# The sums of a wide step: copied by ScalarE and added by GpSimd instead of added by VectorE

## The reference

```python
# layers 0, 2 (wide)
q, k, v = hidden @ Wq, ctx @ Wk, ctx @ Wv            # 16 heads of 64
logits = einsum('bhqd,bhkd->bhqk', q, k) * 64 ** -0.5 + col_bias
probs = softmax(logits, axis=-1)
out = einsum('bhqk,bhkd->bhqd', probs, v)
x = out.reshape(B, HW, 1024) @ Wo + bo + x
# layers 1, 3 (narrow)
xn = rmsnorm(x, norm_w)                              # 16 heads of 16, 4 key/value heads
attn = softmax(einsum('btgrd,bsgd->bgrts', q, k) * 16 ** -0.5, axis=-1)
x = x + einsum('bgrts,bsgd->btgrd', attn, v) @ wo
```

## Time and profile before

| | |
|---|---|
| median of 3 runs | 1727.05 us (1723.91 to 1731.9) |
| profiled execution | 1724.81 us, span 1722.6 us |
| mean granted TensorE clock | 0.967 |
| TensorE (PE) busy | 1599.6 us, 93% |
| VectorE (DVE) busy | 1250.8 us, 73% |
| ScalarE (ACT) busy | 1015.1 us, 59% |
| GpSimd (POOL) busy | 476.2 us, 28% |

### The profile page before, as it was taken

How to read it: one execution, slowest core, us unless ns; L and a number is a source line. 1 busy time by engine, 2 the same in 40 slices (tenths; PEclk the granted TensorE clock), 3 DMA queues, 4 the chain that set the end, 5 groups by cost and what they waited for, 6 DMA issues and landing times.

```text
span 1722.6 us, 29786 instructions
## 1 busy us (share of the span) xinstructions
PE 1599.6 (93%) x10732; PEld 889.0 (52%) x10732; DVE 1250.8 (73%) x2376; ACT 1015.1 (59%) x1721; POOL 476.2 (28%) x354
## 2 busy tenths in 40 slices
PE   7998798999999999999999999999999999999884
PEld 6886444454545454545454454545464545454443
DVE  5474467687878787878777877778787878786551
ACT  2111176667666676667666765676667666666452
POOL 5342402122232322323213222221323132322221
PEclk9898799999999999999999999999999999999886
DMA  7988412241225131513262224322341224030332
GB/s 259 329 298 264 142 33 62 53 83 46 62 49 117 28 85 36 130 26 96 71 135 77 66 60 93 67 56 59 77 87 34 77 57 106 28 88 18 99 112 64
DMA packets 176738, 160.57 MB, mean 93 GB/s; under 512 B 91722, under 2 KB 133066, under 8 KB 175570
## 3 DMA queue, kind: packets, MB, share of 16 engines
q1 hardware_dynamic: 174410, 150.21, 33.3%
q10 hardware_dynamic: 2184, 8.47, 1.2%
HBM read 115.11 MB, written 43.48 MB: 92 GB/s over the span
## 4 chain that ended last, share of the span: by engine, by line
PE 57%; DVE 11%; issue 11%; POOL 4%; ACT 4%; DMA 1%; SPq 1%; ACTq 0%; POOLq 0%; DVEq 0%
PE general L1534 10%; PE general L1653 10%; PE score_ps L1593 5%; PE score_ps L1594 5%; PE out_ps L1608 5%; PE general L1551 3%; PE general L1555 3%; PE general L1613 3%; PE out_ps L1619 3%; PE out_ps L1629 3%; POOL kept L1394 2%; PE score_ps L1582 2%; DVE q_aux L1436 2%; DVE q_aux L1435 2%; DVE a_lo L1470 2%
## 5 line engine op out<-in xcount | busy, mean ns | idle before, releaser
L1445 DVE TENSOR_REDUCE tops<-general 128x2 bf16<-128x308 f32 x1024 | 427.3, 469 | 55.9 <-PE general L1551 33.5
L1289 ACT ACTIVATE probs<-score_ps 128x512 f32<-128x512 f32 x512 | 297.8, 598 | 112.0 <-PE score_ps L1594 100.7
L1394 POOL TENSOR_TENSOR kept<-kept,inv_b 128x512 f32<-128x512 f32 x128 | 171.1, 1358 | 463.0 <-DMA inv_b<-scratch_inverses 463.0
L1432 DVE TENSOR_TENSOR q_pair<-general,q_pair 64x512 fp32r<-64x512 f32 x160 | 109.5, 684 | 168.0 <-ACT q_pair L1277 164.2
L1301 ACT ACTIVATE q_aux<-general 4x512 bf16<-4x512 bf16 x320 | 187.6, 586 | 20.0 <-PE general L1564 15.0
L1276 ACT ACTIVATE q_pair<-general 64x512 fp32r<-64x512 f32 x160 | 94.6, 591 | 154.3 <-PE general L1534 123.7
L1313 ACT ACTIVATE kept<-out_ps 128x512 f32<-128x512 f32 x192 | 104.3, 595 | 85.4 <-PE general L1623 67.0
L1384 POOL TENSOR_TENSOR x_lo<-xn,x_hi 128x1024 fp32r<-128x1024 f32 x31 | 74.0, 2388 | 282.2 <-ACT x_hi L1257 217.7
L1332 ACT ACTIVATE a_hi<-kept 128x512 fp32r<-128x512 f32 x160 | 93.6, 625 | 97.5 <-PE general L1653 49.5
L1594 PE MATMUL score_ps<-q_pair,w_pair 128*128 128x512 f32 x256 | 149.5, 592 | 0.0
L1470 DVE TENSOR_TENSOR a_lo<-kept,a_hi 128x512 fp32r<-128x512 f32 x160 | 125.0, 813 | 32.7 <-ACT a_hi L1332 31.7
(11 more groups left out here) (158 smaller groups left out, 3295.8 us busy)
## 6 DMA issues: line engine op xcount, KB each, us to landing
inv_b<-scratch_inverses SPq DMA_DIRECT2D x128, 256.0 KB, 4.7
w_pair<-scratch_wk_hi SPq DMA_DIRECT2D x32, 256.0 KB, 6.8
x<-scratch_stream SPq DMA_DIRECT2D x16, 512.0 KB, 3.3
inv_n<-scratch_inverses SPq DMA_DIRECT2D x256, 32.0 KB, 1.8
xn<-scratch_stream SPq DMA_DIRECT2D x15, 512.0 KB, 3.3
scratch_stream<-x SPq DMA_DIRECT2D x14, 512.0 KB, 4.6
scratch_wk_hi<-p_kout_hi SPq DMA_DIRECT2D x16, 308.0 KB
p_raw<-in_L_xattn_Wk_dram SPq DMA_DIRECT2D x4, 1024.0 KB, 7.9
```

What stands on the lines that cost most here:

```text
L1289: nc.scalar.activation(dst, score_ps[:, number % 2, :], ACT.Exp, scale=scale).then_inc(act_exp.sem, 1)
L1394: last = nc.gpsimd.tensor_tensor(tiles[i], tiles[i], (inv_b, inv_n)[n % 2][:, i, :], ALU.mult)
L1445: last = nc.vector.tensor_reduce(tops[:, n % 2, sub, 2 * pair:2 * pair + 2], src, AX_X, ALU.max)
```

## The change

For every wide step, ScalarE copies the bank of sums to one of two tiles, `step_sums`, right after its two copies to `kept`. For the second to the fourth step of a chunk GpSimd adds: at the second the two tiles into `wide_sums`, then each next tile to `wide_sums`. VectorE does nothing in `value`. TensorE waits for ScalarE's copy before it uses the bank again, SyncE waits for GpSimd's third addition before it stores the sums, and ScalarE waits, before it fills a tile, for the addition that read the tile last. PLAN is the same.

```diff
-        wide_sums = sb("wide_sums", [P, TOK])
+        wide_sums, step_sums = sb("wide_sums", [P, TOK]), sb("step_sums", [P, 2, TOK])
...
-        dve_sums = Signal(sem("dve_sums"), ("value",), only=WIDE_STEPS, parts=(1,))
+        act_sums = Signal(sem("act_sums"), ("value",), only=WIDE_STEPS, parts=(1,))
+        pool_sums = Signal(sem("pool_sums"), ("value",), only=[n for n in WIDE_STEPS if n % 4], parts=(1,))
...
-        reader = {"value": dve_sums, "query": dve_query, "max": dve_max, "turn": act_turn, "output": dve_output,
+        reader = {"value": act_sums, "query": dve_query, "max": dve_max, "turn": act_turn, "output": dve_output,
...
-                            wait(sp, dve_sums.sem, dve_sums.after(w, "value", 4 * c + 3, 1))
+                            wait(sp, pool_sums.sem, pool_sums.after(w, "value", 4 * c + 3, 1))
...
                         nc.scalar.activation(kept[:, place(tile), :], out_ps[:, tile % 2, :], ACT.Copy).then_inc(act_keep.sem, 1)
+                    if wide(n):
+                        if n % 4 > 1:
+                            before_w, before = it, n - n % 4 + 1
+                        else:
+                            before_w, before = (it, n - 8 + 2) if n >= 8 else (it - 1, n + 8 + 2)
+                        wait(act, pool_sums.sem, pool_sums.after(before_w, what, before, 1))
+                        ps = bank_of((it, what, n, k, 0))
+                        nc.scalar.activation(step_sums[:, n % 2, :], ps, ACT.Copy).then_inc(act_sums.sem, 1)
...
+                elif what == "value":
+
+                    if not wide(n) or k == 0 or n % 4 == 0:
+                        return
+                    wait(pool, act_sums.sem, act_sums.after(it, what, n, k))
+                    if n % 4 == 1:
+                        wait(pool, sums_stored.sem, sums_stored.after(it - (n == 1), "sums", 2 - n // 4, 0))
+                        first = step_sums[:, 0, :]
+                    else:
+                        wait(pool, pool_sums.sem, pool_sums.after(it, what, n - 1, k))
+                        first = wide_sums[:]
+                    nc.gpsimd.tensor_tensor(wide_sums[:], first, step_sums[:, n % 2, :], ALU.add).then_inc(pool_sums.sem, 1)
...
-                elif what == "value":
-
-                    if not wide(n) or k == 0:
-                        return
-                    wait(dve, pe_value.sem, pe_value.after(it, what, n, k))
-                    ps = bank_of((it, what, n, k, 0))
-                    if n % 4 == 0:
-                        wait(dve, sums_stored.sem, sums_stored.after(it - (n == 0), "sums", 2 - n // 4, 0))
-                        nc.vector.tensor_copy(wide_sums[:], ps).then_inc(dve_sums.sem, 1)
-                    else:
-                        wait(dve, dve_sums.sem, dve_sums.after(it, what, n - 1, 1))
-                        nc.vector.tensor_tensor(wide_sums[:], ps, wide_sums[:], ALU.add).then_inc(dve_sums.sem, 1)
```

## The result

The changed kernel took 1761.14 us (median of 4 runs, 1755.24 to 1764.65), the kernel before 1726.33 us in 4 runs beside it. The ratio is 1.0189 with an interval of 1.0164 to 1.0214: about 33 us slower, where 28 were forecast (the two medians are 35 us apart).

The account below looks back on a forecast made before the run. The prediction took TensorE, busy 192.24 of 200 us in a middle stretch, as the bound. It summed 27.5 + 2 + 4 + 1.4 + 2.3 - 9 = +28 us to 1754 us, range 1738 to 1769.

Parts of the forecast that it names:

- The bound, and who waits for whom: Whole kernel: TensorE sets the time; relieving other engines could win only 7.8 us per 200 us, while new waits show fully.
- Steps 10 and 11: GpSimd's additions there delay `scale 1 0` and `scale 1 1`; TensorE loses 1.3 and 4.2 us a window, 27.5 in windows 1-5.
- The chain behind the sums: Sums stored 2.3 us later, reciprocal 1.4 later; hidden in steady windows, +1.4 us in window 0, +2.3 in window 7.
- What comes back: `scale 2 0` no longer meets VectorE's casts, so TensorE's waits for the maxima go: 9 us off, bounds 0 and 14.
- the forecast's -7: From behind step 11 to the next window's step 10, windows 1 to 5: +2 us and -9 us together.
- The rival of more meetings: GpSimd's additions fall on VectorE's casts, about 1.0 us each, 48 us for all: 1790 us, chance 0.05.
- The small terms: Each window: banks of sums come free 1.0 us later, partly won back; +0.4 us net, bounds -0.5 and +2.
- The ends: First and last windows: +1.4 us in window 0, +4 in window 6, +2.3 in window 7.
- The sign: Whole kernel: slower with chance 0.85, same 0.09, faster 0.06.

Follow-up runs that it names:

- the run made for it: Kernel before, with GpSimd holding `scale 2 0` until VectorE has done the casts of the next window's `query 0 0` (windows 1 to 5): ratio 1.0013.

## Why the prediction was right, and where it was wrong

**The bound, and who waits for whom.** Right. VectorE got 50 us of relief and the time rose by 33: with TensorE busy 96% of a middle stretch, less work elsewhere can't show, while a wait that reaches TensorE does.

**Steps 10 and 11: right in mechanism and size.** Forecast 5.5 us a window and 27.5 in all, measured 5.1 and 25.6. The waits of ScalarE were 2.34 and 4.23 us for 2.7 and 4.2, in all five windows; TensorE's behind step 11 was 3.13 for 4. The runs with moved scalings take away 4.3 of the 5.1; the 0.8 that stay also appear with the copies alone, and belong to the bank.

**The chain behind the sums: right where it looked, incomplete.** The delay was right (SyncE's store 2.25 us later behind the copies, 2.3 forecast), and so was "in the steady windows this disappears behind the 4.2 us that TensorE has lost just before" for chunk 2: its reciprocals in windows 1 to 5 never wait. The waits at the ends came as forecast too: 1.5 us in window 0 (1.4), 3.6 in window 6 (3 to 4), 2.6 in window 7 (2.3). What the prediction put at nothing without a word is chunk 0 of the steady windows, behind step 3, where no loss stands in front: waits of 1.0 to 2.5 us, 0.3 to 0.9 us at step 5. Its 3.7 us for the chain were too few: measured is a term between 7 and 16 us, as worked out above, of which the traces place 4 to 5 us in window 6 and behind it, and don't place the rest for certain.

**What comes back: wrong.** The 9 us were taken from VectorE's meetings with GpSimd. They did get rarer: the casts' groups fell from 185.4 to 170.5 us (87.4 and 83.1 in the changed kernel). But TensorE's waits for the maxima went only from 8.7 to 7.8 us, and the run made for it won nothing. That the rest of windows 1 to 5 shows -5.6 us, near the forecast's -7, is no support: the kernel with the additions alone shows the same -5.6, and each holds its clock's share (+6.6 in the changed kernel) and whatever the windows' own slack took back, which I can't separate. The rival of more meetings is out: VectorE's maxima take 470 ns for 469, and its `a_lo` 811 for 813.

**The small terms.** Forecast +0.4 us a window, with -0.5 and +2 as bounds. The copies alone cost 9 us in all, inside these bounds; 0.8 us a window of it is at step 11, which the prediction had not among the steps that want the bank. In the changed kernel TensorE won 0.5 us at step 1 in windows 2 to 6, as forecast.

**The ends.** Window 6 cost 6.1 us for 4, window 7 0.3 for 2.3. Window 0 cost 5.2 for 1.4, 3.7 of it between steps 9 and 10, but its share varied by several us between the runs (2.4 us at this place with the last step on VectorE, 2.0 and 0 in other kernels). In window 1, 4.1 us were lost between steps 1 and 2: 3.4 with the additions alone, 3.4 and 2.3 with the squares moved, 1.5 with the copies alone, and 1.5 also in the kernel with `scale 2 0` kept back, which has neither copies nor additions. What does it stays open.

**The clock.** Not foreseen; 6.6 us of the account are its share, but removing it there didn't move the time clear of the noise.

By place, the profiled execution misses the forecast by 12 us (40 for 28): 2 in the preparation, 10 in window 0 and ahead of step 10 of window 1, and no more than some 2 in any other row. The medians' +33 is nearer than this. In the rows that agree, the pairs do so for the reason given; the -5.6 for -7 and window 7 do so by errors that cancel. The sign and the first cause are shown; the total being that near is partly luck.

## What to carry to other kernels

An engine that is busy 28% is still one queue: before work is moved to it, ask what stands behind the new instruction, and how early that used to run. A short addition that waits for late data takes from everything behind it the lead that it had. Here it paid to move those additions whose result wasn't wanted yet, to leave the last one of each group, on which a chain of transfers hangs, with the engine that can read the bank at once, and to put the queued work of the receiving engine ahead. Done so, this change was 0.9978 (0.9965 to 0.9992) of the kernel before instead of 1.0189. And where a chain gets longer, look at every place where it runs: here chunk 2's delay was hidden by another loss, and chunk 0's wasn't.

## What the runs showed of the hardware

In the changed kernel a wait of 3.13 us on TensorE was followed by a low granted clock in four windows of five (0.61 in the slice of 4 us shown above for window 4), and not in the fifth. In the kernel with moved squares, the clock was already low before the wait of 5.39 us ended at 1098.48:

```profile
1090.00:1096.00 6.00, 3.09 (x17) 2.22 (x15) 0.48 (x2) 0.00 (x0) 2.21 (x2) 1.00 1.11 184
1096.00:1100.00 4.00, 1.52 (x8) 0.20 (x8) 1.76 (x3) 3.65 (x7) 0.28 (x1) 0.56 1.30 198
```

Had it fallen only then, the slice from 1096 to 1100 would show a mean of 0.81, and it shows 0.56. Twelve matmuls in the wait of the changed kernel, 2.75 us of it, kept the clock up at this place in all five windows. That the 6.6 us so won didn't show in the time of the program is the part I hadn't expected.
